# Two heads of transposed probabilities in one DMA transpose, in a decoder layer on one core

## The chip, the core and the metric

The kernel runs on one core of a Trainium2 chip. The metric is the device time of one execution, in microseconds (us), on that core. The kernel before takes 2261.62 us in the median of three runs. The engines are called PE (TensorE matmul), PEld (its weight loads), DVE (VectorE), ACT (ScalarE), POOL (GpSimd) and SP (SyncE, which here issues every DMA).

## The reference

One decoder layer, for 32 batches of 256 tokens of width 256: a causal self-attention with 8 query heads of 128 and one shared key and value head (stage a), a cross-attention with 16 heads of 16 (stage b), and a feed-forward part with 8 gated experts of which the 2 best count, and a shared one (stage c).

```python
x = x + _L0_attn_ref(_layernorm(x), Wq, Wk, Wv, Wo)
x = x + _L0_xattn_ref(_layernorm(x), ctx, ctx, fside, fside, mask, fside_SxS, ...)
x = x + _L0_ffn_ref(_layernorm(x), gate_w, lb_bias, w1, w2, cfc, cproj)

# _L0_xattn_ref, for each batch and each of H = 16 heads of D = 16:
scores = jnp.einsum('bhtd,bhsd->bhts', q, k) * scale
scores = scores + attn_mask[None, None, :, :]
scores = jnp.where(pad, -jnp.inf, scores)
scores = scores + spatial_bias + directional_bias
probs = jax.nn.softmax(scores, axis=-1)
out = jnp.einsum('bhts,bhsd->bhtd', probs, v)
```

## The kernel before

The batches go through the three stages in a software pipeline. Each engine has a list in `ORDERS`, written out by hand, of steps `name:argument@lag`; the engine walks through its list once for each iteration, and a step with lag L works on the batch of L iterations ago. So one iteration of each list is one batch's worth of work from stages a, b and c of different batches, and its length sets the time: 32 batches, and six more iterations in which the pipeline fills and empties. Between the engines there are only semaphores.

In the cross-attention a head j of a batch goes this way, with 256 x 256 probabilities:

- PE makes the scores (`b_s`), DVE adds the bias and takes the negative maximum (`b_s`, line 838), ACT takes the exponential into a PSUM bank (`b_s`, lines 656 and 658).
- ACT rounds it to float16, the "hi" part (`b_p_hi`, line 666), and DVE writes the remainder, the "lo" part (`b_p_lo`, line 845), both into slot `j % DEPTH` of `b_p2` (`DEPTH = 4`).
- SP issues a DMA transpose of the slot, 128 partitions x 1024 columns of float16 (256 KB), into slot `head % RING` of `b_pT` (`RING = 4`); the step is `b_pT:j`, the function `b_pT_load`, line 423. Ahead of it SP waits for DVE's remainder and for PE's product of the head four before, which has read that slot.
- PE multiplies the transposed probabilities with the values (`b_pv:j`, line 1115, 12 small matmuls), once the transpose has landed.
- ACT, when it comes to head j + 4, waits for the landing of head j's transpose ahead of `b_p_hi`, for it writes the same slot of `b_p2`.

After `b_pv:15` DVE divides by the sums (`b_n`, line 857), PE projects the output (`b_o`, `b_wo`), and the layer norm of stage c follows, which the expert products (`c_f1`, `c_f2`) wait for. In PE's list `b_pv:14` and `b_pv:15` stand side by side.

SP's list holds, beside the 16 transposes of a batch, its other DMAs: eight loads of bias (512 KB each, `b_load`), the loads of x and of the context, the store of the result (`c_f2:8`), and, at the end of a batch, the store of q (`b_store_q`, line 390) and k (`b_store_k`, line 383) into a scratch in DRAM and 16 loads that stack them again. All run in one queue (q1). `b_pT:15` has lag 5 and stands at the head of the list, behind `b_store_q`; `b_load:7` and the context's load (`b_split_q`) are the last steps of the list, so that they are issued just ahead of it.

Of the kernel before, what the change touches and what calls it, by code (L numbers as in the profile page):

```python
# [31 lines left out]
BH, BD = 16, 16  # L32
# [4 lines left out]
DEPTH = 4  # L37
RING = 4
# [28 lines left out]
def order(text):  # L67
# [6 lines left out]

ORDERS = {name: order(text) for name, text in dict(
    sync="""
        b_store_q:0@4 b_pT:15@5 b_store_k:0@4 b_stack_q:0@4 b_stack_k:0@4 b_pT:0@4 c_f2:8@6 b_pT:1@4 b_load:0@4
        b_mask:0@4 b_load:1@4 b_pT:2@4 a_ln:0@3 b_pT:3@4 b_load:2@4 b_pT:4@4 b_pT:5@4 b_pT:6@4 b_load:3@4
        b_pT:7@4 b_pT:8@4 b_pT:9@4 b_load:4@4 b_load:5@4 b_pT:10@4 b_pT:11@4 b_load:6@4 a_T:0@2 w_load:4@2
        w_load:5@2 w_load:6@2 w_load:7@2 w_load:8@2 w_load:9@2 w_load:10@2 w_load:11@2 w_load:12@2 w_load:13@2  # L80
        w_load:14@2 w_load:15@2 w_load:16@2 w_load:17@2 w_load:18@2 w_load:19@2 b_pT:12@4 b_pT:13@4 b_pT:14@4
        b_load:7@4 b_split_q:0@3""",
    gpsimd="""
        c_f1:1@6 c_lo:1@6 b_res:0@5 c_f1:2@6 c_lo:2@6 b_comb:6@5 c_f1:3@6 b_comb:7@5 c_lo:3@6 c_f1:4@6
        b_comb:8@5 b_comb:9@5 c_lo:4@6 c_f1:5@6 b_comb:10@5 b_comb:11@5 c_lo:5@6 b_comb:12@5 a_ln:0@3
# [51 lines left out]
def build(nc, x_d, ctx_d, bias_d, mask_d, pad_d, wpair_d, cst_d, bq_d, bk_d, bv_d, bo_d, lb_d, stk_d, out_d):  # L137
    with ExitStack() as ctx:
        def sb(name, shape, dt=F32):
            return ctx.enter_context(nc.sbuf_tensor(name, shape, dt))  # L140
# [4 lines left out]
        def sem(name):  # L145
            return ctx.enter_context(nc.semaphore(name))
# [12 lines left out]
        b_mask = sb("b_mask", [P, CT * T])  # L159
# [58 lines left out]
        b_p2 = sb("b_probs_hi_lo", [P, DEPTH, CT, 2, T], F16)  # L218
        b_pT = sb("b_probsT_hi_lo", [P, RING, CT, 2, CT, P], F16)
# [62 lines left out]
        b_s_ps, b_t_ok, b_e_ok = sem("b_scores_in_psum"), sem("b_neg_scores_ready"), sem("b_exp_ready")  # L282
        b_i_ok = sem("b_inv_ready")
        b_ph_ok, b_p_ok = sem("b_probs_hi_ready"), sem("b_probs_hi_lo_ready")
        b_pT_ok = [sem(f"b_probsT_loaded{n}") for n in range(RING)]
        b_pv_ps, b_of_ok, b_oT_ps = sem("b_pv_in_psum"), sem("b_out_ready"), sem("b_oT_in_psum")
        b_oh_ok, b_o_ok = sem("b_oT_hi_ready"), sem("b_oT_ready")
        b_res_ok, b_wo_ps, x2_ok = sem("x1_bo_ready"), sem("b_wo_in_psum"), sem("x2_ready")
# [36 lines left out]
        def _(sp):  # L325
# [92 lines left out]
            def b_pT_load(b, j):  # L418

                head = b * BH + j  # L420
                sp.wait_ge(b_p_ok, head + 1)
                sp.wait_ge(b_pv_ps, max(head + 1 - RING, 0))
                sp.dma_start_transpose(b_pT[:, head % RING, :, :, :, :].rearrange("p c r s t -> p (c r s) t"),
                                       b_p2[:, j % DEPTH, :, :, :].rearrange("p c r t -> p (c r t)")).then_inc(
                                           b_pT_ok[head % RING], 16)

            def b_mask_row(b, _):

# [4 lines left out]
            def c_f2(b, e):  # L433
                if e == NX - 1:
# [3 lines left out]
            iterations(sp, "sync", dict(w_load=w_load, a_ln=a_ln, a_T=a_T, b_load=b_load, b_split_q=b_split_q,  # L438
                                b_mask=b_mask_row, c_f2=c_f2, b_store_k=b_store_k, b_store_q=b_store_q,
                                b_stack_k=b_stack_k, b_stack_q=b_stack_q, b_pT=b_pT_load))  # L440
            sp.wait_ge(s_out, 16 * BATCHES)

# [109 lines left out]
        def _(act):  # L552
# [16 lines left out]
            def ln_xn(st, x):  # L569
                def step(b, _):  # L570
                    L = ln[st]
                    act.wait_ge(s_nmr[st], after(b, 1, 1))
                    act.wait_ge(s_lnT[st], after(b, 1, 0))
                    for c in range(CT):
                        act.activation(L["xn"][:, c, :], x[:, c, :], ACT.Identity, bias=L["nmr"][:, c:c + 1],
                                       scale=L["rstd"][:, c:c + 1]).then_inc(s_xn[st], 1)
                return step

            def ln_hi(st, free_sem, per_batch):
                def step(b, _):  # L580
                    L = ln[st]
                    act.wait_ge(s_lnT[st], after(b, 1, 1))
                    act.wait_ge(free_sem, after(b, per_batch, 0))
                    act.activation(L["hi"][:, :, :], ln_bank[st][:, :].rearrange("p (k t) -> p k t", k=CD),
                                   ACT.Copy).then_inc(s_xh[st], 1)
                return step
# [74 lines left out]
            def b_p_hi(b, j):  # L661
                act.wait_ge(b_e_ok, after(b, BH, j + 1))
                free = b * BH + j - DEPTH
                if free >= 0:
                    act.wait_ge(b_pT_ok[free % RING], 16 * (free // RING + 1))
                act.activation(b_p2[:, j % DEPTH, :, 0, :], ps_bp[:, :].rearrange("p (c t) -> p c t", c=CT),  # L666
                               ACT.Copy).then_inc(b_ph_ok, 1)

# [17 lines left out]
            def c_sq(b, e):  # L686
# [5 lines left out]
                                           a_T=ln_hi("a", a_q_ps, 4), b_T=ln_hi("b", b_q_ps, 1), c_T=ln_hi("c", c_f1_ps, NX),  # L692
                                 a_ln=ln_xn("a", x_ln), b_ln=ln_xn("b", x1), c_ln=ln_xn("c", x2),
                                 a_kv=a_kv, a_q=a_q_hi, a_s=a_s, a_n=a_n, a_pt=a_pt, a_pv=a_pv, b_kv=b_kv, b_q=b_q,
                                 b_v=b_v_hi, b_s=b_s, b_p=b_p_hi, b_o=b_o_hi, c_gate=c_gate, c_f1=c_f1, c_sq=c_sq))


# [265 lines left out]
        def _(pe):  # L963
# [140 lines left out]

            def b_pv(b, j):
                u = (b * BH + j) % RING
                pe.wait_ge(b_pT_ok[u], 16 * ((b * BH + j) // RING + 1))
                if j == 0:
                    pe.wait_ge(x2_ok, after(b, 1, 0))
                    pe.wait_ge(b_vl_ok, after(b, 1, 1))  # L1110
                for c in range(CT):
                    at = c * D + j * BD
                    for s in range(CT):
                        for n, (part, v) in enumerate([(0, b_vh), (0, b_vl), (1, b_vh)]):
                            last = pe.matmul(ps_bm[:, at:at + BD], b_pT[:, u, c, part, s, :],  # L1115
                                             v[:, s, j * BD:(j + 1) * BD], start=(s == 0 and n == 0),
                                             stop=(s == CT - 1 and n == 2))
                last.then_inc(b_pv_ps, 1)
# [37 lines left out]
            def c_f2(b, e):  # L1156
# [6 lines left out]
                for c in range(CT):  # L1163
# [78 lines left out]
```

## Time and profile before

| what | value |
|---|---|
| time, median of 3 runs | 2261.62 us (2259.73 to 2263.55) |
| the profiled execution | 2262.71 us, of which its span is 2260.9 us |
| PE, PEld busy | 92%, 80% |
| ACT, DVE, POOL busy | 90%, 82%, 79% |
| DMA queue q1, share of 16 engines | 72.4% |
| mean granted TensorE clock | 0.980 |

A share is an average over the whole span. PE is busy nine tenths of it, and in a trace of matmuls that overlap this does not mean that it works at its peak. What ends the small waits between its work has to be read from the views that list waits, and from the order of time within one batch.

### The profile page before, as it was taken

How to read it: one execution, taken by the hardware profiler on the slowest of the kernel's cores; microseconds unless marked ns; L12 is line 12 of the kernel's file. 1: busy time of each engine (PE TensorE's matmuls, PEld its weight loads, DVE VectorE, ACT ScalarE, POOL GpSimd, SP SyncE). 2: the span in 40 equal slices, each digit the busy share in tenths (PEclk: the TensorE clock that was granted, in tenths of full speed). 3: DMA queues.
4: the chain of work that ended last, by engine and by line, in shares of the span. 5: the costliest groups of instructions: out<-in, count | busy, mean ns of one | idle time of the engine just before them, and what ended most of it. 6: DMA issues, size and time to landing. Idle time of an engine off the chain costs nothing.

```text
span 2260.9 us, 73067 instructions
## 1 busy us (share of the span) xinstructions
PE 2077.8 (92%) x24128; PEld 1806.0 (80%) x24128; DVE 1860.7 (82%) x6768; ACT 2024.0 (90%) x5937; POOL 1780.8 (79%) x1899
## 2 busy tenths in 40 slices
PE   4679999999999999999999999999999999999877
PEld 2568888888888888888888888888888888888755
DVE  4578888888888888888888888888888888888763
ACT  5689999999999999999999999999999999999862
POOL 2358888888888887888888888888888888777863
PEclk9789999999999999999999999999999999999987
DMA  4388778778877779767776887677788777789860
GB/s 142 114 191 175 159 156 172 162 170 188 172 157 154 175 157 175 183 162 169 163 173 156 182 185 164 165 169 169 161 176 187 159 168 165 169 152 183 172 129 15
DMA packets 711784, 367.16 MB, mean 162 GB/s; under 512 B 561392, under 2 KB 659952, under 8 KB 711408
## 3 DMA queue, kind: packets, MB, share of 16 engines
q1 hardware_dynamic: 711408, 362.50, 72.4%
q8 instruction: 193, 3.16, 0.6%
q14 instruction: 183, 1.50, 0.2%
HBM read 202.98 MB, written 25.17 MB: 101 GB/s over the span
## 4 chain that ended last, share of the span: by engine, by line
PE 61%; issue 11%; POOL 10%; ACT 8%; DMA 5%; DVE 5%; SPq 1%; ACTq 0%; DVEq 0%; POOLq 0%
PE ps_c_hidden L978 15%; PE ps_a_misc L978 14%; PE ps_c_out L978 14%; PE ps_b_misc L1115 5%; DMA b_probsT_hi_lo<-b_probs_hi_lo 5%; PE ps_b_scores L1101 3%; POOL bias L522 3%; PE ps_a_misc L1057 3%; ACT c_relu L684 2%; PE ps_a_scores L1038 2%; ACT ps_b_probs L658 2%; POOL ctxT_hi L488 2%; ACT a_qT_hi L603 1%; POOL a_qT_lo L480 1%; POOL ctxT_lo L491 1%
## 5 line engine op out<-in xcount | busy, mean ns | idle before, releaser
L522 POOL TENSOR_TENSOR bias<-bias,b_mask 128x512 f32<-128x512 f32 x512 | 645.0, 1274 | 6.2 <-DMA bias<-in_bias 5.8
L838 DVE CUSTOM_DVE_ANT_0 b_neg_scores<-ps_b_scores,bias 128x256 f32<-128x256 f32 x1024 | 391.2, 419 | 68.3 <-POOL bias L522 34.2
L845 DVE TENSOR_TENSOR b_probs_hi_lo<-ps_b_probs,b_probs_hi_lo 128x512 f16<-128x512 f32 x512 | 351.7, 687 | 107.3 <-ACT b_probs_hi_lo L666 104.9
L543 POOL TENSOR_TENSOR c_hidden_lo<-c_hidden,c_hidden_hi 128x512 f16<-128x512 f32 x288 | 335.1, 1163 | 48.4 <-issue 32.8
L978 PE MATMUL ps_c_hidden<-c_xT_hi,w_hi 128*128 128x256 f16 x1152 | 317.2, 275 | 19.9 <-ACT c_relu L684 19.9
L536 POOL TENSOR_TENSOR c_hidden<-c_relu 128x512 f32<-128x512 f32 x288 | 299.7, 1041 | 32.4 <-ACT c_relu L684 13.1
L978 PE MATMUL ps_c_out<-w_hi,c_hidden_hi 128*128 128x256 f16 x1152 | 315.6, 274 | 9.9 <-DVE acc L949 9.9
L978 PE MATMUL ps_c_hidden<-c_xT_hi,w_lo 128*128 128x256 f16 x1152 | 316.8, 275 | 0.0
L978 PE MATMUL ps_c_hidden<-c_xT_lo,w_hi 128*128 128x256 f16 x1152 | 316.7, 275 | 0.0
L978 PE MATMUL ps_c_out<-w_hi,c_hidden_lo 128*128 128x256 f16 x1152 | 315.9, 274 | 0.0
L978 PE MATMUL ps_c_out<-w_lo,c_hidden_hi 128*128 128x256 f16 x1152 | 315.8, 274 | 0.0
L666 ACT ACTIVATE b_probs_hi_lo<-ps_b_probs 128x512 f16<-128x512 f32 x512 | 303.3, 592 | 9.3
L656 ACT ACTIVATE ps_b_probs<-b_neg_scores,b_neg_max 128x256 f32<-128x256 f32 x512 | 245.5, 480 | 55.2 <-DVE b_probs_hi_lo L845 51.1
L658 ACT ACTIVATE ps_b_probs<-b_neg_scores,b_neg_max 128x256 f32<-128x256 f32 x512 | 240.0, 469 | 0.0
L480 POOL TENSOR_TENSOR a_qT_lo<-a_qT,a_qT_hi 128x512 f16<-128x512 f32 x128 | 148.5, 1160 | 115.2 <-ACT a_qT_hi L603 111.8
L949 DVE SCALAR_TENSOR_TENSOR acc<-ps_c_out,g_weights,acc 128x256 f32<-128x256 f32 x512 | 220.7, 472 | 21.6 <-PE ps_c_out L978 21.6
L1115 PE MATMUL ps_b_misc<-b_v_hi,b_probsT_hi_lo 128*128 128x16 f16 x4096 | 218.0, 170 | 21.1 <-DMA b_probsT_hi_lo<-b_probs_hi_lo 21.0
L1115 PEld LDWEIGHTS ps_b_misc<-b_v_hi,b_probsT_hi_lo 128*128 128x128 f16 x4096 | 203.4, 96 | 26.9 <-DMA b_probsT_hi_lo<-b_probs_hi_lo 22.7
L1115 PE MATMUL ps_b_misc<-b_v_lo,b_probsT_hi_lo 128*128 128x16 f16 x2048 | 194.7, 169 | 0.0
L689 ACT ACTIVATE c_hidden_hi<-c_relu 128x512 f16<-128x512 f32 x288 | 180.9, 628 | 6.9 <-PE ps_c_out L978 6.8
L684 ACT ACTIVATE c_relu<-ps_c_hidden 128x512 f32<-128x512 f32 x288 | 170.7, 593 | 14.5 <-PE ps_c_hidden L978 14.5
L978 PE MATMUL ps_a_misc<-a_xT_hi,w_hi 128*128 128x256 f16 x576 | 159.5, 277 | 11.4 <-DVE a_v_lo L752 6.1
(194 smaller groups left out, 7491.0 us busy)
## 6 DMA issues: line engine op xcount, KB each, us to landing
bias<-in_bias SPq DMA_DIRECT2D x256, 512.0 KB, 4.2
q_stack<-qk_scratch SPq DMA_DIRECT2D x256, 64.0 KB, 2.5
x_ln<-in_x SPq DMA_DIRECT2D x32, 256.0 KB, 4.4
ctxT<-in_ctx SPq DMA_DIRECT2D x32, 256.0 KB, 4.4
x<-in_x SPq DMA_DIRECT2D x32, 256.0 KB, 5.5
qk_scratch<-b_qT_hi_lo SPq DMA_DIRECT2D x32, 256.0 KB, 4.5
qk_scratch<-b_kT_hi_lo SPq DMA_DIRECT2D x32, 256.0 KB, 3.7
k_stack_even<-qk_scratch SPq DMA_DIRECT2D x128, 64.0 KB, 2.5
```

The lines of the kernel that those rows point to most:

```text
L522: gp.tensor_tensor(part, part, b_mask[:, :], ALU.add).then_inc(b_c_ok, 1)
L536: gp.tensor_tensor(c_h[:, :], c_r[:, e % 2, :], c_r[:, e % 2, :], ALU.mult).then_inc(c_sq_ok, 1)
L543: gp.tensor_tensor(c_hl[:, u, :], c_h[:, :], c_hh[:, u, :], ALU.subtract).then_inc(c_h_ok, 1)
L656: act.activation(ps_bp[:, 0:T], b_t[:, u, 0, :], ACT.Exp, bias=b_mx[:, u, 0:1], scale=-1.0, accum_out=b_sum[:, 0, j:j + 1])
L658: act.activation(ps_bp[:, T:2 * T], b_t[:, u, 1, :], ACT.Exp, bias=b_mx[:, u, 1:2], scale=-1.0, accum_out=b_sum[:, 1, j:j + 1]).then_inc(b ...
L666: act.activation(b_p2[:, j % DEPTH, :, 0, :], ps_bp[:, :].rearrange("p (c t) -> p c t", c=CT), ACT.Copy).then_inc(b_ph_ok, 1)
L684: act.activation(c_r[:, e % 2, :], ps_c1[:, :], ACT.Relu, scale=R_UP / W_UP).then_inc(c_r_ok, 1)
L838: last = dve.tensor_tensor_reduce(out=b_t[:, u, c, :], in0=ps_bs[:, c * T:(c + 1) * T], in1=bias[:, slot, at:at + T], scale=-2.0, scalar=3 ...
L845: dve.tensor_tensor(b_p2[:, j % DEPTH, :, 1, :], ps_bp[:, :].rearrange("p (c t) -> p c t", c=CT), b_p2[:, j % DEPTH, :, 0, :], ALU.subtrac ...
L949: last = dve.scalar_tensor_tensor(out=acc[:, c, :], in0=ps_c2[:, c * D:(c + 1) * D], scalar=g_we[:, c, e - 1:e], in1=acc[:, c, :], op0=ALU ...
L978: last = pe.matmul(out, stat(s, k), mov(m, k), start=(k == 0 and n == 0), stop=(k == chunks - 1 and n == len(parts) - 1))
L1115: last = pe.matmul(ps_bm[:, at:at + BD], b_pT[:, u, c, part, s, :], v[:, s, j * BD:(j + 1) * BD], start=(s == 0 and n == 0), stop=(s == CT ...
```

## The change

Two neighbouring heads, 2m and 2m + 1, go in one DMA transpose of 128 partitions x 2048 columns. SP's list keeps the odd steps `b_pT:1` to `b_pT:15` where they stood and drops the even ones. The semaphore `b_pT_ok` is one for a pair of slots, two in all in place of four. `b_pv` of either head of a pair, and `b_p_hi` of the heads four later, wait for the pair.

```diff
     sync="""
-        b_store_q:0@4 b_pT:15@5 b_store_k:0@4 b_stack_q:0@4 b_stack_k:0@4 b_pT:0@4 c_f2:8@6 b_pT:1@4 b_load:0@4
...
-        w_load:14@2 w_load:15@2 w_load:16@2 w_load:17@2 w_load:18@2 w_load:19@2 b_pT:12@4 b_pT:13@4 b_pT:14@4
-        b_load:7@4 b_split_q:0@3""",
+        b_store_q:0@4 b_pT:15@5 b_store_k:0@4 b_stack_q:0@4 b_stack_k:0@4 c_f2:8@6 b_pT:1@4 b_load:0@4
...
+        w_load:17@2 w_load:18@2 w_load:19@2 b_pT:13@4 b_load:7@4 b_split_q:0@3""",
...
-        b_pT_ok = [sem(f"b_probsT_loaded{n}") for n in range(RING)]
+        b_pT_ok = [sem(f"b_probsT_loaded{n}") for n in range(RING // 2)]
...
                 head = b * BH + j
+                pair = head // 2 % (RING // 2)
                 sp.wait_ge(b_p_ok, head + 1)
                 sp.wait_ge(b_pv_ps, max(head + 1 - RING, 0))
-                sp.dma_start_transpose(b_pT[:, head % RING, :, :, :, :].rearrange("p c r s t -> p (c r s) t"),
-                                       b_p2[:, j % DEPTH, :, :, :].rearrange("p c r t -> p (c r t)")).then_inc(
-                                           b_pT_ok[head % RING], 16)
+                sp.dma_start_transpose(b_pT[:, 2 * pair:2 * pair + 2, :, :, :, :].rearrange("p u c r s t -> p (u c r s) t"),
+                                       b_p2[:, j % DEPTH - 1:j % DEPTH + 1, :, :, :].rearrange("p u c r t -> p (u c r t)")).then_inc(
+                                           b_pT_ok[pair], 16)
...
-                    act.wait_ge(b_pT_ok[free % RING], 16 * (free // RING + 1))
+                    act.wait_ge(b_pT_ok[free // 2 % (RING // 2)], 16 * (free // RING + 1))
...
-                pe.wait_ge(b_pT_ok[u], 16 * ((b * BH + j) // RING + 1))
+                pe.wait_ge(b_pT_ok[u // 2], 16 * ((b * BH + j) // RING + 1))
```

SP at the end of a batch, before: the three transposes in one row are those of heads 12, 13 and 14, the single one is that of head 15, and between them stand the last load of bias, the load of the context and the store of q.

```order
L361 DMA x_ln<-in_x 128x512 [waits a_xT_in_psum]
L423 DMA_TRANSPOSE b_probsT_hi_lo<-b_probs_hi_lo 128x8x128 [waits b_pv_in_psum,b_probs_hi_lo_ready] x3
L370 DMA bias<-in_bias 128x1024 [waits b_neg_scores_ready]
L376 DMA ctxT<-in_ctx 128x512 [waits ctx_lo_ready]
L390 DMA qk_scratch<-b_qT_hi_lo 128x4x256 [waits b_q_lo,b_q_stack_loaded]
L423 DMA_TRANSPOSE b_probsT_hi_lo<-b_probs_hi_lo 128x8x128 [waits b_pv_in_psum,b_probs_hi_lo_ready]
L383 DMA qk_scratch<-b_kT_hi_lo 128x4x256 [waits b_k_lo,b_k_stack_loaded]
```

The same place in the changed kernel:

```order
L360 DMA x_ln<-in_x 128x512 [waits a_xT_in_psum]
L423 DMA_TRANSPOSE b_probsT_hi_lo<-b_probs_hi_lo 128x16x128 [waits b_pv_in_psum,b_probs_hi_lo_ready]
L369 DMA bias<-in_bias 128x1024 [waits b_neg_scores_ready]
L375 DMA ctxT<-in_ctx 128x512 [waits ctx_lo_ready]
L389 DMA qk_scratch<-b_qT_hi_lo 128x4x256 [waits b_q_lo,b_q_stack_loaded]
L423 DMA_TRANSPOSE b_probsT_hi_lo<-b_probs_hi_lo 128x16x128 [waits b_pv_in_psum,b_probs_hi_lo_ready]
L382 DMA qk_scratch<-b_kT_hi_lo 128x4x256 [waits b_k_lo,b_k_stack_loaded]
```

Head 14 has moved from ahead of the bias, context and q transfers to behind them, and the load of bias no longer stands behind a transpose that waits for head 14's remainder.

ACT in the middle of a batch, before; `b_probsT_loaded` is the semaphore of the slot's transpose, and the rows left out are other stages' steps:

```order
L666 ACTIVATE b_probs_hi_lo<-ps_b_probs 128x2x256 [waits b_probsT_loaded0,b_exp_ready]
...
L666 ACTIVATE b_probs_hi_lo<-ps_b_probs 128x2x256 [waits b_probsT_loaded1,b_exp_ready]
...
L666 ACTIVATE b_probs_hi_lo<-ps_b_probs 128x2x256 [waits b_probsT_loaded2,b_exp_ready]
L684 ACTIVATE c_relu<-ps_c_hidden 128x512 [waits c_hidden_hi_ready,c_square_ready,c_hidden_in_psum]
...
L666 ACTIVATE b_probs_hi_lo<-ps_b_probs 128x2x256 [waits b_probsT_loaded3,b_exp_ready]
```

The same rows in the changed kernel:

```order
L666 ACTIVATE b_probs_hi_lo<-ps_b_probs 128x2x256 [waits b_probsT_loaded0,b_exp_ready]
...
L666 ACTIVATE b_probs_hi_lo<-ps_b_probs 128x2x256 [waits b_probsT_loaded0,b_exp_ready]
...
L666 ACTIVATE b_probs_hi_lo<-ps_b_probs 128x2x256 [waits b_probsT_loaded1,b_exp_ready]
L684 ACTIVATE c_relu<-ps_c_hidden 128x512 [waits c_hidden_hi_ready,c_square_ready,c_hidden_in_psum]
...
L666 ACTIVATE b_probs_hi_lo<-ps_b_probs 128x2x256 [waits b_probsT_loaded1,b_exp_ready]
```

No step of ACT has moved; the first head of a pair now waits for a transpose that starts with the second head's remainder, one head later than before.

## Rows read from the trace of the kernel before

**Rows 1.** The page: the chain that ended last, by engine, shares of the span.

```profile
PE 61%; issue 11%; POOL 10%; ACT 8%; DMA 5%; DVE 5%; SPq 1%; ACTq 0%; DVEq 0%; POOLq 0%
```

**Rows 2.** Waits of the whole span: total us, times, longest us.

```profile
PE ps_b_misc L1115 <- DMA b_probsT_hi_lo<-b_probs_hi_lo: 21.0, 18, 2.1
```

**Rows 3.** DVE's line 851, once per batch, in batches 7, 8, 19, 20: ns, then start.

```profile
L851 DVE RECIPROCAL b_inv<-b_sum x1: 349/349/349, 615.7 to 615.7; 128x32 f32<-128x32 f32 x1
L851 DVE RECIPROCAL b_inv<-b_sum x1: 346/346/346, 683.3 to 683.3; 128x32 f32<-128x32 f32 x1
L851 DVE RECIPROCAL b_inv<-b_sum x1: 350/350/350, 1412.4 to 1412.4; 128x32 f32<-128x32 f32 x1
L851 DVE RECIPROCAL b_inv<-b_sum x1: 348/348/348, 1478.0 to 1478.0; 128x32 f32<-128x32 f32 x1
```

**Rows 4.** Timeline of PE, first matmul of `b_pv:15` of batch 7; in brackets, idle time ahead.

```profile
624.48 0.18 PE L1115 MATMUL ps_b_misc<-b_v_hi,b_probsT_hi_lo 128*128 128x16 f16 x1 [1.91 <-DMA b_probsT_hi_lo<-b_probs_hi_lo]
```

**Rows 5.** Timeline of SP, end of batch 16: transposes of heads 13, 14, 15 and between.

```profile
1210.67 1.24 SPq L423 DMA_TRANSPOSE b_probsT_hi_lo<-b_probs_hi_lo  x1
...
1213.39 1.78 SPq L423 DMA_TRANSPOSE b_probsT_hi_lo<-b_probs_hi_lo  x1
1215.22 0.57 SPq L370 DMA_DIRECT2D bias<-in_bias  x1
1215.85 0.42 SPq L376 DMA_DIRECT2D ctxT<-in_ctx  x1
1216.40 0.38 SPq L390 DMA_DIRECT2D qk_scratch<-b_qT_hi_lo  x1
1216.88 1.50 SPq L423 DMA_TRANSPOSE b_probsT_hi_lo<-b_probs_hi_lo  x1
```

**Rows 6.** Timeline of PE, batch 16: first matmuls of `b_pv:14` and of `b_pv:15`.

```profile
1221.72 0.17 PE L1115 MATMUL ps_b_misc<-b_v_hi,b_probsT_hi_lo 128*128 128x16 f16 x1
...
1222.34 0.18 PE L1115 MATMUL ps_b_misc<-b_v_hi,b_probsT_hi_lo 128*128 128x16 f16 x1 [0.17 <-DMA b_probsT_hi_lo<-b_probs_hi_lo]
```

**Rows 7.** All transposes: ns min/median/max of the issue; us from issue to landing.

```profile
L423 SPq DMA_TRANSPOSE b_probsT_hi_lo<-b_probs_hi_lo x512: 1231/1252/3742, 111.4 to 2204.7; - x171
...
DMA to landing us min/median/max: 3.0/3.5/7.9
```

**Rows 8.** Landing of head 15's transpose alone, in batch 19, then in batch 7.

```profile
DMA to landing us min/median/max: 4.8/4.8/4.8
DMA to landing us min/median/max: 7.4/7.4/7.4
```

**Rows 9.** DMA issues: KB each, median us from issue to landing.

```profile
bias<-in_bias SPq DMA_DIRECT2D x256, 512.0 KB, 4.2
...
x_ln<-in_x SPq DMA_DIRECT2D x32, 256.0 KB, 4.4
...
qk_scratch<-b_qT_hi_lo SPq DMA_DIRECT2D x32, 256.0 KB, 4.5
qk_scratch<-b_kT_hi_lo SPq DMA_DIRECT2D x32, 256.0 KB, 3.7
```

**Rows 10.** Timelines of DVE and POOL, batch 16: head 15's scores and remainder; q's remainder.

```profile
1212.24 0.42 DVE L838 CUSTOM_DVE_ANT_0 b_neg_scores<-ps_b_scores,bias 128x256 f32<-128x256 f32 x1
1215.54 0.68 DVE L845 TENSOR_TENSOR b_probs_hi_lo<-ps_b_probs,b_probs_hi_lo 128x512 f16<-128x512 f32 x1
1214.94 1.16 POOL L505 TENSOR_TENSOR b_qT_hi_lo<-b_qT,b_qT_hi_lo 128x512 f16<-128x512 f32 x1 [1.44 <-issue]
```

**Rows 11.** Timelines, batch 16: SP's transpose of head 7, ACT's head 10.

```profile
1194.32 1.38 SPq L423 DMA_TRANSPOSE b_probsT_hi_lo<-b_probs_hi_lo  x1
...
1199.19 0.60 ACT L666 ACTIVATE b_probs_hi_lo<-ps_b_probs 128x512 f16<-128x512 f32 x1
```

**Rows 12.** Timelines, batch 16: SP's transpose of head 11, PE's first matmul of head 10.

```profile
1205.96 1.23 SPq L423 DMA_TRANSPOSE b_probsT_hi_lo<-b_probs_hi_lo  x1
...
1211.25 0.17 PE L1115 MATMUL ps_b_misc<-b_v_hi,b_probsT_hi_lo 128*128 128x16 f16 x1
```

More of the change, by code:

```diff
@@ L76 @@
     sync="""
-        b_store_q:0@4 b_pT:15@5 b_store_k:0@4 b_stack_q:0@4 b_stack_k:0@4 b_pT:0@4 c_f2:8@6 b_pT:1@4 b_load:0@4
-        b_mask:0@4 b_load:1@4 b_pT:2@4 a_ln:0@3 b_pT:3@4 b_load:2@4 b_pT:4@4 b_pT:5@4 b_pT:6@4 b_load:3@4
-        b_pT:7@4 b_pT:8@4 b_pT:9@4 b_load:4@4 b_load:5@4 b_pT:10@4 b_pT:11@4 b_load:6@4 a_T:0@2 w_load:4@2
-        w_load:5@2 w_load:6@2 w_load:7@2 w_load:8@2 w_load:9@2 w_load:10@2 w_load:11@2 w_load:12@2 w_load:13@2
-        w_load:14@2 w_load:15@2 w_load:16@2 w_load:17@2 w_load:18@2 w_load:19@2 b_pT:12@4 b_pT:13@4 b_pT:14@4
-        b_load:7@4 b_split_q:0@3""",
+        b_store_q:0@4 b_pT:15@5 b_store_k:0@4 b_stack_q:0@4 b_stack_k:0@4 c_f2:8@6 b_pT:1@4 b_load:0@4
+        b_mask:0@4 b_load:1@4 a_ln:0@3 b_pT:3@4 b_load:2@4 b_pT:5@4 b_load:3@4 b_pT:7@4 b_pT:9@4 b_load:4@4
+        b_load:5@4 b_pT:11@4 b_load:6@4 a_T:0@2 w_load:4@2 w_load:5@2 w_load:6@2 w_load:7@2 w_load:8@2
+        w_load:9@2 w_load:10@2 w_load:11@2 w_load:12@2 w_load:13@2 w_load:14@2 w_load:15@2 w_load:16@2
+        w_load:17@2 w_load:18@2 w_load:19@2 b_pT:13@4 b_load:7@4 b_split_q:0@3""",
     gpsimd="""
```

## The prediction

> **What bounds the kernel now.** I read the chain that ended last first, because five engines between 79% and 92% busy do not say which of them waits for what. It is PE for 61% of the span, and DMA for 5% [rows 1]; the reader is to see there that a transfer stands on the path at all, 5% of 2260.9 us being 113 us, or 3.5 us in each of 32 batches. The view of waits then says which: PE's product of probabilities and values waits for the DMA transpose 18 times, 21.0 us in all, 2.1 us at most [rows 2]. Eighteen times in 32 batches is about once in every second batch, so I looked for one head of the 16 at which it happens, and it is head 15.
>
> Whether such a wait costs time is read from the length of a batch. In batch 19 no such wait stands, and DVE's line 851 comes again after 1478.0 - 1412.4 = 65.6 us; in batch 7 PE waits 1.91 us ahead of `b_pv:15`, and the next line 851 comes after 683.3 - 615.7 = 67.6 us [rows 3, 4]. The batch is longer by 2.0 us, all of the wait. It is paid in full: DVE's division, the output projection and stage c's layer norm follow head 15's product.
>
> Why head 15: SP issues its transpose at 1216.88, right behind the load of bias (512 KB), the load of the context and the store of q, three transfers within 1.7 us [rows 5]. PE starts `b_pv:14` at 1221.72, 4.84 us after that issue. `b_pv:15` starts at 1222.34 after 0.17 us of waiting; it could have started at 1222.17, 5.29 us after the issue, 0.45 us behind `b_pv:14` [rows 6]. A transpose lands after 3.0 us at best and 3.5 us in the median [rows 7]; head 15's took 4.8 us in batch 19, which is in time, and 7.4 us in batch 7, which is not [rows 8].
>
> **The change part by part.** *A longer transfer.* The issue of 8 blocks of 128 columns takes 1.23 to 1.25 us where nothing holds it up [rows 7]. No row shows 16 blocks. The nearest row for an upper bound is that issue: if blocks are made one after the other, a pair's last block leaves, and lands, 1.24 us later. The nearest for the lower bound are plain loads, where 512 KB land after 4.2 us and 256 KB after 4.4 [rows 9]: twice the bytes, no time. An issue of plain transfers takes 0.38 to 0.57 us whatever their size [rows 5], so a transpose's 1.24 us cannot be a fixed cost of issuing alone. I take 1.24 us and keep 0 for the range.
>
> *A weighing.* The Trainium skill ("DMA: Bandwidth & Descriptors", section "Anatomy of one DMA", fitted there on GpSimd's path) gives one transfer a fixed 2.0 us and its bytes over 436 GB/s, and its section "Rules for kernel authors" says to join small transfers. By that the second 256 KB would add an estimated 0.6 us in place of 1.24, and the sum below would be +4.5 us in place of +21.6. The trace's 3.0 us for the shortest transpose is above the 2.6 us that the formula gives for 256 KB.
>
> *Less traffic just ahead.* Head 14's transpose, which now leaves from 1213.39 to 1215.17, goes; the load of bias and the context's load, which stand behind it, need only the scores of head 15, done at 1212.66, and a free queue [rows 5, 10]. The pair 12, 13 is issued when head 13's is now, at 1210.67, and holds the queue for 2.5 us by the price above, to 1213.15. So both loads leave about 2.0 us earlier than at 1215.22 and 1215.85. The store of q does not: POOL's remainder of q ends at 1216.10 [rows 10], 0.3 us ahead of the store's issue. It then has almost no traffic in front. What that is worth shows in two stores of the same size: q's lands after 4.5 us, k's, behind a gap, after 3.7 [rows 9]. So 0.8 us. Bounds: nothing, and 1.45 us, the amount by which the slower 4.5 us exceeds the shortest transpose of 3.0 us.
>
> *Head 14 waits for head 15.* This is the edit's price on the path. Now `b_pv:14` is done before `b_pv:15` may start; after it, both wait for one landing and run one behind the other, so that `b_pv:15` starts 0.45 us after the landing [rows 6]. The pair's issue cannot move forward, for head 15's remainder ends at 1216.22 [rows 10], behind which only the store of q stands.
>
> *The sum at this place.* In the 18 batches that wait [rows 2]: 0.45 + 1.24 - 0.8 = 0.89 us more, 16.0 us in all. In the other 14: a landing of 4.8 us [rows 8] becomes 5.24 us, 0.40 us over the 4.84 us at which PE wants `b_pv:14`, 5.6 us in all. Together +21.6 us.
>
> *The other pairs,* with 1.24 us on top of their odd head's landing. ACT's head 10 writes the slot of head 6, whose pair is issued with head 7's transpose at 1194.32 and lands, by the median 3.5 us, at 1199.06; ACT starts at 1199.19 [rows 7, 11]. It is covered by 0.13 us, thin cover; without it, each us that the landing is late stops ACT, and PE's expert products want its rectified values next. PE's head 10 is wanted at 1211.25, and its pair, issued with head 11's at 1205.96, lands at 1210.70 [rows 7, 12]; the cover is 0.55 us. Landings scatter (3.0 to 7.9 us), so these two lose a little: an estimate of 0.1 us a batch, 3 us in all. The same issue order frees SP at the end of batches such as 16, where head 15's transpose left 0.66 us after the remainder it needs (1216.88 - 1216.22), of which 0.3 us is the store of q that the queue held up; at 0.3 us in a third of the batches that is 3 us back. I set these two against each other. SP's other issues keep their order, and a queue that now waits in fewer places costs nothing that a row shows.
>
> Against the profiled execution, 2262.71 us, of which 2260.9 is the span, the sum is 2284.3 us; that execution stands 1.1 us over the median of the three runs, so the forecast is 2283 us.
>
> **The rivals.** *Faster: the queue clears.* If the pair lands no later than one head does today (0 for the longer transfer) and the loads' head start is worth 0.8 us, each waiting batch wins 0.8 - 0.45 = 0.35 us, 6 us in all; with 1.45 us it wins 1.0 us, 18 us, of the 21.0 us that there are. Between them, 2250 us. It decides at a landing 4.84 us after the issue: if most pairs are there by then, PE waits at neither head. For it: the plain loads in rows 9. Against: the issue time in rows 7.
>
> *The same:* a longer transfer at about 0.5 us, between the bounds. Each waiting batch then costs 0.45 + 0.5 - 0.8 = 0.15 us, 2.7 us in all, and the others 4.8 - 0.3 = 4.5 us, in time: 2264 us. The formula cited above would give nearly this.
>
> *Much slower: no relief.* If head 15's landing is late for something other than the loads in front, it stays, and all of 0.45 + 1.24 = 1.69 us comes on top in 18 batches (30 us), and 4.8 + 1.24 - 4.84 = 1.2 us in 14 (17 us): 2309 us. For it: 4.8 us in one batch and 7.4 us in another behind the same three transfers [rows 8], which a queue of fixed length does not explain. With ACT's head 10 late by 0.5 us in every batch it would be 16 us more.
>
> **How the numbers follow.** Forecast, slower by about 1%: 0.45; much slower: 0.17; the same: 0.18; faster: 0.20. A change of 0.2%, 4.5 us, is about what a measurement of this kernel can tell from none. So faster 0.20, same 0.18, slower 0.62. The range runs from the middle of the faster case, 2250 us, to the much slower case and a little of ACT's share, 2315 us; the likeliest case alone spans 2270 to 2298 us, a transfer price of 0.9 to 1.5 us.
>
> **What would show it.** Right: an issue of about 2.5 us for 16 blocks; PE's waits for the transpose rise from 21 us to about 43, in most batches, now ahead of `b_pv:14`; the store of q lands after about 3.7 us; batches of 65.6 us become rare. Wrong: an issue well under 2 us, or pairs of heads 14 and 15 that land within 4.8 us. New waits of ACT's line 666 for the transpose would mean that the slots of `b_p2`, not PE's last heads, set the price.

## The result and the profile after

The changed kernel takes 2309.97 us (2304.36 to 2311.97, 4 runs), the kernel before, run beside it, 2261.77 us: a ratio of 1.0209, 95% interval 1.019 to 1.0229. It is slower by 48 us, where 21 had been forecast. The profiled execution took 2309.93 us with a span of 2308.1.

The page of the changed kernel, chain that ended last, by engine:

```profile
PE 41%; DMA 15%; issue 13%; POOL 12%; ACT 11%; DVE 7%; SPq 1%; DVEq 0%; ACTq 0%; POOLq 0%
```

DMA stood at 5% [rows 1] and now holds 15% of the path. The waits of the changed kernel (us in all, times, longest) say whose:

```profile
PE ps_b_misc L1115 <- DMA b_probsT_hi_lo<-b_probs_hi_lo: 47.6, 40, 3.7
DVE b_out L857 <- PE ps_b_misc L1115: 43.7, 31, 3.8
ACT b_probs_hi_lo L666 <- DMA b_probsT_hi_lo<-b_probs_hi_lo: 14.4, 16, 1.6
```

PE waits 47.6 us for the transposes in place of 21.0 [rows 2], and ACT has a wait that it did not have at all, for the slots of `b_p2`. (DVE's 43.7 us, 23.9 before, are ahead of its division, line 857, which waits for the last product: in the main the same waits, seen one step on.) PE's and ACT's together are 62.0 us against 21.0, a rise of 41 us; the span rose by 47.2. Sorted by head, from the idle time ahead of each head's first matmul in PE's timeline: before, 19.2 us ahead of head 15 and 1.8 ahead of head 12; now 35.3 ahead of head 14, 5.9 ahead of head 10, 5.0 ahead of head 12, 1.4 ahead of head 2. ACT's 14.4 us stand ahead of head 10 (12.1), 6 and 14.

All pairs of the changed kernel: ns min/median/max of the issue, then us from issue to landing.

```profile
L423 SPq DMA_TRANSPOSE b_probsT_hi_lo<-b_probs_hi_lo x256: 1317/2670/5212, 113.8 to 2252.0; - x128
...
DMA to landing us min/median/max: 4.2/4.9/8.4
```

The shortest landing rose from 3.0 to 4.2 us [rows 7], by 1.2 us, near the 1.24 of the forecast. The shortest issue barely rose, from 1231 to 1317 ns, but the median is 2670 ns, more than two single issues of 1252. Summed over the trace, the transposes' issues take 678 us in place of 743: half as many issues in nine tenths of the time. What had been two issues, apart from each other, now stands in one piece where only the second had stood.

The end of batch 12 of the changed kernel, timeline of SP from pair 12, 13 to pair 14, 15, and below it PE's first matmul of `b_pv:14`:

```profile
965.91 3.20 SPq L423 DMA_TRANSPOSE b_probsT_hi_lo<-b_probs_hi_lo  x1
969.16 0.58 SPq L369 DMA_DIRECT2D bias<-in_bias  x1
969.78 0.43 SPq L375 DMA_DIRECT2D ctxT<-in_ctx  x1
971.25 0.38 SPq L389 DMA_DIRECT2D qk_scratch<-b_qT_hi_lo  x1
971.73 4.49 SPq L423 DMA_TRANSPOSE b_probsT_hi_lo<-b_probs_hi_lo  x1
...
977.89 0.18 PE L1115 MATMUL ps_b_misc<-b_v_hi,b_probsT_hi_lo 128*128 128x16 f16 x1 [0.97 <-DMA b_probsT_hi_lo<-b_probs_hi_lo]
```

In this batch the load of bias leaves 2.57 us ahead of the last transpose. Over batches 1 to 30 the median is 3.0 us, in the kernel before 2.0: 1.0 us earlier, not the 2.0 of the forecast, in the main because the issue of pair 12, 13 takes 3.3 us in the median (3.20 here) and not 2.5. PE takes up `b_pv:14` 6.16 us after the issue, with a wait of 0.97 us ahead of it; in batch 16 of before it started after 4.84 us without one [rows 6].

One long wait, batch 22 of the changed kernel: PE's first matmul of `b_pv:14` in the timeline, and DVE's line 851 ahead of it and in the next batch, by its line.

```profile
1647.71 0.19 PE L1115 MATMUL ps_b_misc<-b_v_hi,b_probsT_hi_lo 128*128 128x16 f16 x1 [3.50 <-DMA b_probsT_hi_lo<-b_probs_hi_lo]
```

```profile
L851 DVE RECIPROCAL b_inv<-b_sum x1: 349/349/349, 1637.5 to 1637.5; 128x32 f32<-128x32 f32 x1
L851 DVE RECIPROCAL b_inv<-b_sum x1: 345/345/345, 1709.6 to 1709.6; 128x32 f32<-128x32 f32 x1
```

Line 851 of the next batch starts at 1709.6, 72.1 us later: 6.5 us over the 65.6 of a batch without a wait [rows 3], for a wait of 3.5. A single long wait can cost more than itself, and here the granted clock of TensorE accounts for the rest. The same batch in four stretches, PE alone (start and end, us, PE's busy time and instructions, granted clock as a share of 2.4 GHz, DMA share, GB/s): up to the wait, the wait, behind it, the rest.

```profile
1637.50:1644.21 6.71, 6.71 (x84) 1.00 1.15 249
1644.21:1647.71 3.50, 0.01 (x2) 0.87 0.80 203
1647.71:1653.62 5.91, 5.91 (x52) 0.50 0.50 137
1653.62:1709.60 55.98, 53.90 (x624) 1.00 0.64 146
```

The clock falls to its lower level, 1.2 GHz, while PE waits, and stays there for 5.91 us after the wait. If PE's work takes twice as long there, that is an estimated 3.0 us on top of the 3.5, which together are the 6.5. The same view from 200 to 2100 us, that is, without the pipeline's filling and emptying, before and after the change:

```profile
200.00:2100.00 1900.00, 1822.29 (x21599) 1.00 0.77 168
200.00:2100.00 1900.00, 1799.23 (x21162) 0.99 0.74 165
```

In that stretch the kernel before has no time at 1.2 GHz at all. The changed kernel has five falls, 24 us together, each one in or within 2 us behind a wait of 1.6 to 3.5 us for the last pair: an estimate of up to 12 us lost, beside the waits themselves.

DMA issues of the changed kernel (KB each, median us to landing), those of [rows 9]:

```profile
bias<-in_bias SPq DMA_DIRECT2D x256, 512.0 KB, 4.4
...
x_ln<-in_x SPq DMA_DIRECT2D x32, 256.0 KB, 4.7
...
qk_scratch<-b_qT_hi_lo SPq DMA_DIRECT2D x32, 256.0 KB, 3.6
qk_scratch<-b_kT_hi_lo SPq DMA_DIRECT2D x32, 256.0 KB, 3.4
```

The store of q lands after 3.6 us in place of 4.5, as forecast from k's 3.7: the traffic ahead of it did thin out.

### The profile page after: what moved, and what is told of

Read it like the earlier page. It is cut to its first block, busy times and chain, and to the rows that moved or that the text cites. A ratio compares the mean times of both kernels' runs of the same rounds, so it can differ in the third digit from the quotient of the medians.

```text
span 2308.1 us, 72555 instructions
## 1 busy us (share of the span) xinstructions
PE 2094.8 (91%) x24128; PEld 1807.4 (78%) x24128; DVE 1862.1 (81%) x6768; ACT 2025.2 (88%) x5937; POOL 1780.6 (77%) x1899
## 4 chain that ended last, share of the span: by engine, by line
PE 41%; DMA 15%; issue 13%; POOL 12%; ACT 11%; DVE 7%; SPq 1%; DVEq 0%; ACTq 0%; POOLq 0%
DMA b_probsT_hi_lo<-b_probs_hi_lo 14%; PE ps_c_hidden L978 10%; PE ps_c_out L978 9%; PE ps_a_misc L978 8%; POOL bias L522 4%; PE ps_b_misc L1115 4%; PE ps_b_scores L1101 2%; ACT c_relu L684 2%; PE ps_a_misc L1057 2%; ACT ps_b_probs L658 2%; ACT ps_b_probs L656 2%; DVE b_neg_scores L838 2%; ACT a_qT_hi L603 1%; POOL b_qT_hi_lo L505 1%; POOL ctxT_hi L488 1%
## 5 line engine op out<-in xcount | busy, mean ns | idle before, releaser
L536 POOL TENSOR_TENSOR c_hidden<-c_relu 128x512 f32<-128x512 f32 x288 | 299.7, 1041 | 31.5 <-ACT c_relu L684 12.1
L666 ACT ACTIVATE b_probs_hi_lo<-ps_b_probs 128x512 f16<-128x512 f32 x512 | 303.2, 592 | 23.6 <-DMA b_probsT_hi_lo<-b_probs_hi_lo 14.4
L1115 PE MATMUL ps_b_misc<-b_v_hi,b_probsT_hi_lo 128*128 128x16 f16 x4096 | 216.2, 170 | 48.0 <-DMA b_probsT_hi_lo<-b_probs_hi_lo 47.6
```

The costliest lines, as they stand in the source:

```text
L536: gp.tensor_tensor(c_h[:, :], c_r[:, e % 2, :], c_r[:, e % 2, :], ALU.mult).then_inc(c_sq_ok, 1)
```

## The experiments

In these kernels a list `SPLIT` names the pairs (0 for heads 0 and 1, to 7 for heads 14 and 15) whose two heads are moved singly again, each in its old place of SP's list and on a semaphore of its own; `landed(head)` gives the semaphore and count that a head's readers wait for. Every time is a median beside runs of the kernel before on the same chip, 2261 to 2263 us.

**First question: which pair costs.** Theory A put the loss at the last pair, as the forecast did; rival B at the seven others.

*Heads 14 and 15 single again, the others joined.*

```diff
+SPLIT = [7]
...
-        w_load:17@2 w_load:18@2 w_load:19@2 b_pT:13@4 b_load:7@4 b_split_q:0@3""",
+        w_load:17@2 w_load:18@2 w_load:19@2 b_pT:13@4 b_pT:14@4 b_load:7@4 b_split_q:0@3""",
...
+                if j // 2 in SPLIT:
+                    sp.dma_start_transpose(b_pT[:, head % RING, :, :, :, :].rearrange("p c r s t -> p (c r s) t"),
+                                           b_p2[:, j % B_DEPTH, :, :, :].rearrange("p c r t -> p (c r t)")).then_inc(
+                                               landed(head)[0], 16)
+                    return
```

> Heads 14 and 15 go in two transposes again, head 14 ahead of the last load of bias as in the kernel before; the other seven pairs stay joined. Theory A (the loss of 48 us sits at the last pair, where head 14 has been put behind three other transfers and its product behind one landing): about 29 us come back, 2275 to 2285 us, and PE's waits for the transpose fall from 47.6 to 25 to 32 us. Rival B (a joined transfer costs about the same wherever it stands, through ACT's slots and PE's other heads): no more than an eighth to a quarter comes back, 2298 us or over.

Measured: 2297.02 us, ratio 1.0139 (1.0118 to 1.016). PE waits 38.4 us, of them 26.1 at head 15; ACT 14.6. Most of the loss is still there; the time is 12 us above theory A's range and 1 us below rival B's.

*Only heads 14 and 15 joined.*

```diff
+SPLIT = [0, 1, 2, 3, 4, 5, 6]
```

> The other way round: only heads 14 and 15 are joined, the other 14 heads go singly in the places that they have in the kernel before. Theory A: nearly all of its share, 2285 to 2297 us, with PE waiting for head 14 in most batches. Rival B: 2262 to 2272 us.

Measured: 2270.86 us, ratio 1.0036 (1.0017 to 1.0055); PE waits 24.0 us, ACT none. The last pair alone costs about 8 us, and PE's wait at head 14 is 22.8 us, only 3.6 more than head 15's before. Theory A falls: the other seven cost 34 us by the run above. The two together are 42 of the 48 us; the rest comes only when all pairs are joined.

*Two single transposes, one behind the other, at each odd head's place.* This keeps the place and the bytes of the joined transfer, but the first head's landing is told on its own.

```diff
+                    for n in (j - 1, j):
+                        sp.dma_start_transpose(b_pT[:, (b * BH + n) % RING, :, :, :, :].rearrange("p c r s t -> p (c r s) t"),
...
```

> At the place of every joined transpose, and after the same waits, two single ones are issued one behind the other, each with its own semaphore; so both heads still wait for the second, and the same bytes go at the same time, but the first head's landing is told on its own. Theory A, in the form that the place in the queue counts: head 14 is still behind the other transfers; only the 0.45 us of its product and the first halves' later landings come back, 2275 to 2292 us. Rival C (the one landing for two heads is the whole cost, the place nothing): 2262 to 2270 us.

Measured: 2290.34 us, ratio 1.0112 (1.0093 to 1.0132); PE waits 33.9 us (head 14 19.7, head 15 10.1), ACT 2.1. Rival C falls: with the one landing for two heads taken away, 27 of the 48 us stay. This run leaves two things as they were in the changed kernel, the even head's transpose held back to the odd head's place and the two transfers in one row, and does not tell one from the other. ACT's wait at head 10 goes from 12.1 to 0.6 us, PE's from 5.9 to none: these were waits of an even head for the joint landing.

*Pairs 3 and 7 split (heads 6, 7, 14 and 15).*

```diff
+SPLIT = [3, 7]
```

> As e1_last_split, and the pair of heads 6 and 7 is split too, so that ACT's head 10 waits for head 6 alone, which is issued one load earlier. Theory A with ACT's 14.4 us of waits for the transpose as a cost in full: 8 to 14 us under e1_last_split. If ACT has slack there: within 4 us of e1_last_split.

Measured: 2289.84 us (2277.98 to 2297.56), ratio 1.0101 (1.0067 to 1.0135). In the profiled run, one of the long ones (2297.18), ACT's wait at head 10 is gone, and PE's at head 15 is 31.6 us. Against the first run ACT waits 10.5 us less and PE 5.6 us more, so that in this run half of what pair 3 gave back was lost again. By the medians 7 us are won against the first run, a little under the 8 to 14 of the theory, where the runs lie 20 us apart.

**Second question: why head 15 waits more when heads 10 to 13 are joined.** In the first run above head 15's own transpose was single again, yet its wait was 26.1 us in place of 19.2.

*Pairs 6 and 7 split: heads 12 to 15 single as before the change.*

```diff
+SPLIT = [6, 7]
```

> The transposes of heads 12 to 15 are single again, those of heads 0 to 11 are joined as in the changed kernel. Theory, each joined pair costs where its own slack is short: the end of the batch is then as before (the loads of bias and context leave about 2 us ahead of head 15's issue, PE's waits at heads 12 and 15 about 21 us), and what is left is PE's head 10 and head 2 (some 7 us of waits) and ACT's head 10 (12 us), so PE waits about 28 us, ACT about 12 us, and the time is 2275 to 2285 us. Rival, any joined transfer holds up the one queue and with it all that follows, head 15 too: PE's waits stay at 35 us or more and the time at 2290 us or more.

Measured: 2297.41 us, ratio 1.0153 (1.0113 to 1.0194); PE waits 39.0 us, head 15 32.0 of it; ACT 11.9. The rival holds: a joined pair costs far behind itself.

*Only heads 0 to 5, 8 and 9 joined.*

```diff
+SPLIT = [3, 5, 6, 7]
```

> Only heads 0 to 5, 8 and 9 are joined (four pairs); 6, 7 and 10 to 15 are single as before the change. ACT's slot for head 10 and PE's heads 10, 12, 14 and 15 then hang on single transposes. Theory, a joined pair costs only where its slack is short: PE waits 21 to 24 us, ACT none, and the time is 2260 to 2268 us, level with the kernel before. Rival, any joined transfer costs through the shared queue: about 5 us for each pair, so 2275 to 2285 us.

Measured: 2264.89 us, ratio 1.0034 (1.0011 to 1.0056); PE waits 17.9 us, ACT 2.4. Within the theory's range, though the interval says a loss of 0.1 to 0.6%. So it is not any pair; pairs 3 and 5 make the difference.

*Only heads 10 and 11 joined.*

```diff
+SPLIT = [0, 1, 2, 3, 4, 6, 7]
...
-        b_pT:7@4 b_pT:8@4 b_pT:9@4 b_load:4@4 b_load:5@4 b_pT:10@4 b_pT:11@4 b_load:6@4 a_T:0@2 w_load:4@2
+        b_pT:7@4 b_pT:8@4 b_pT:9@4 b_load:4@4 b_load:5@4 b_pT:11@4 b_load:6@4 a_T:0@2 w_load:4@2
```

(The lines taken away and added are of the kernel before.)

> Only heads 10 and 11 are joined; the fourteen others are single, in the order of the kernel before. Theory, the queue on SP has no slack between head 11 and head 15: the pair's issue takes 0.7 us more than head 11's, all that follows on SP moves back, and head 15's wait grows from 19 us to about 30 although nothing of head 15 changed; with 5 us of PE's waits at head 10 that is 2272 to 2280 us. Rival, a pair costs only at its own heads: 5 us at head 10, head 15 as before, 2262 to 2268 us.

Measured: 2291.76 us, ratio 1.0123 (1.0101 to 1.0145): one joined pair of eight costs 28 us, more than the theory's 11 to 19 (30 us by the medians). Head 15's wait is 32.1 us, head 10's 5.0, ACT has none. The timeline of SP in batch 18 of this kernel (start, us of the issue), from the pair to head 15:

```profile
1346.26 2.03 SPq L442 DMA_TRANSPOSE b_probsT_hi_lo<-b_probs_hi_lo  x1
1348.33 0.91 SPq L383 DMA_DIRECT2D bias<-in_bias  x1
1349.29 0.44 SPq L374 DMA_DIRECT2D x_ln<-in_x  x1
1349.83 1.24 SPq L438 DMA_TRANSPOSE b_probsT_hi_lo<-b_probs_hi_lo  x1
1351.17 2.57 SPq L438 DMA_TRANSPOSE b_probsT_hi_lo<-b_probs_hi_lo  x1
1353.83 2.19 SPq L438 DMA_TRANSPOSE b_probsT_hi_lo<-b_probs_hi_lo  x1
1356.07 0.57 SPq L383 DMA_DIRECT2D bias<-in_bias  x1
1356.69 0.51 SPq L389 DMA_DIRECT2D ctxT<-in_ctx  x1
1357.34 0.38 SPq L403 DMA_DIRECT2D qk_scratch<-b_qT_hi_lo  x1
1357.82 1.48 SPq L438 DMA_TRANSPOSE b_probsT_hi_lo<-b_probs_hi_lo  x1
```

The same stretch of the kernel before, the same batch, from head 11 to head 15:

```profile
1337.48 1.23 SPq L423 DMA_TRANSPOSE b_probsT_hi_lo<-b_probs_hi_lo  x1
1338.77 0.57 SPq L370 DMA_DIRECT2D bias<-in_bias  x1
1339.39 0.43 SPq L361 DMA_DIRECT2D x_ln<-in_x  x1
1340.40 1.25 SPq L423 DMA_TRANSPOSE b_probsT_hi_lo<-b_probs_hi_lo  x1
1342.19 2.00 SPq L423 DMA_TRANSPOSE b_probsT_hi_lo<-b_probs_hi_lo  x1
1344.91 1.23 SPq L423 DMA_TRANSPOSE b_probsT_hi_lo<-b_probs_hi_lo  x1
1346.19 0.57 SPq L370 DMA_DIRECT2D bias<-in_bias  x1
1346.81 0.62 SPq L376 DMA_DIRECT2D ctxT<-in_ctx  x1
1347.72 0.38 SPq L390 DMA_DIRECT2D qk_scratch<-b_qT_hi_lo  x1
1348.20 1.80 SPq L423 DMA_TRANSPOSE b_probsT_hi_lo<-b_probs_hi_lo  x1
```

Count from the first row of each. The pair's issue is 0.80 us longer, the load of bias behind it 0.34; layer norm's x leaves 1.12 us later, and behind it the issues of heads 13 and 14 take 2.57 and 2.19 us in place of 2.00 and 1.23. SP has no idle time left here: from 1349.83 to 1356.07 one issue follows the other, where there were gaps of 0.58, 0.54 and 0.72 us. The two loads end their issue 0.99 us later (10.94 us after the first row in place of 9.95), the store of q leaves 0.84 us later, and so does head 15's transpose, at 11.56 us in place of 10.72. It is the late issue that counts: over batches 1 to 30 head 15's transpose leaves 1.03 us after the remainder that it needs, 0.55 before (means), and then lands after 5.75 us, as before (5.73). The transposes' waits rise by 17 of the 28 us. Of the rest, the clock is a part: between 200 and 2100 us it falls to 1.2 GHz five times, 17 us in all, each time in or within 2 us behind a wait at head 15 of 1.7 us or more, an estimate of up to 8.5 us.

*Only heads 6 and 7 joined.*

```diff
+SPLIT = [0, 1, 2, 4, 5, 6, 7]
```

> Only heads 6 and 7 are joined; the others are single. Theory, what this pair costs is ACT's head 10, which overwrites head 6's slot: ACT waits 10 to 12 us there, PE's waits are those of the kernel before (21 us), and the time is 2270 to 2276 us. Rival, ACT's wait is taken up by the slack behind it: the wait shows, and the time stays at 2259 to 2264 us.

Measured: 2276.24 us, ratio 1.0078 (1.0051 to 1.0106). Waits of this kernel:

```profile
ACT b_probs_hi_lo L685 <- DMA b_probsT_hi_lo<-b_probs_hi_lo: 16.4, 19, 2.0
PE ps_b_misc L1134 <- DMA b_probsT_hi_lo<-b_probs_hi_lo: 14.8, 17, 2.4
```

The theory's mechanism holds against the rival: the slot wait is paid for, all of it at head 10, which overwrites head 6. Its numbers were missed: ACT's wait is 16.4 us for 10 to 12, PE's 14.8 for 21, and the time stands just above its range.

**Third question: is a wait paid one for one, and does the cause lie in the loads ahead of the last transpose.**

*The kernel before, with the loads of bias and context behind head 15's transpose in SP's list.*

```diff
-        b_store_q:0@4 b_pT:15@5 b_store_k:0@4 b_stack_q:0@4 b_stack_k:0@4 b_pT:0@4 c_f2:8@6 b_pT:1@4 b_load:0@4
+        b_store_q:0@4 b_pT:15@5 b_load:7@5 b_split_q:0@4 b_store_k:0@4 b_stack_q:0@4 b_stack_k:0@4 b_pT:0@4 c_f2:8@6 b_pT:1@4 b_load:0@4
...
-        w_load:14@2 w_load:15@2 w_load:16@2 w_load:17@2 w_load:18@2 w_load:19@2 b_pT:12@4 b_pT:13@4 b_pT:14@4
-        b_load:7@4 b_split_q:0@3""",
+        w_load:14@2 w_load:15@2 w_load:16@2 w_load:17@2 w_load:18@2 w_load:19@2 b_pT:12@4 b_pT:13@4 b_pT:14@4""",
```

> The kernel before, with single transposes; in SP's list the loads of bias and context for the next batch stand right behind head 15's transpose instead of ahead of it. Theory, the loads in front make head 15's landing late: its median landing falls from 5.2 us to below 4.5, PE's waits for it from 19 us to below 8, and the time is 2240 to 2252 us. Rival, the late landings have another cause: PE's waits stay at 15 us or more and the time at 2258 to 2264 us. If the loads are now late for the next batch, a new wait for bias or context shows and the time is above 2265 us.

Measured: 2245.23 us, ratio 0.9934 (0.9912 to 0.9957): faster than both kernels, and the theory's number. Its waits for transposes, the end of batch 16 on SP's timeline, and the landing of the transpose seen there:

```profile
PE ps_b_misc L1114 <- DMA b_probsT_hi_lo<-b_probs_hi_lo: 1.2, 1, 1.2
```

```profile
1208.81 0.39 SPq L389 DMA_DIRECT2D qk_scratch<-b_qT_hi_lo  x1
1209.29 1.29 SPq L422 DMA_TRANSPOSE b_probsT_hi_lo<-b_probs_hi_lo  x1
1210.64 0.57 SPq L369 DMA_DIRECT2D bias<-in_bias  x1
1211.26 0.42 SPq L375 DMA_DIRECT2D ctxT<-in_ctx  x1
```

```profile
DMA to landing us min/median/max: 3.3/3.3/3.3
```

With the loads behind it, head 15's transpose lands after 3.3 us, and PE waits for head 15 in no batch; the one wait left stands ahead of head 12. The chain of this kernel has 1% of DMA.

*The same move in the changed kernel.*

> The changed kernel with the same move: the loads of bias and context behind the transpose of heads 14 and 15. Theory, the loads in front make the last landing late: pair 14 and 15 lands after about 4.5 us in place of 6.2, PE's waits at head 14 fall from 35 us to about 10, and the time is 2275 to 2290 us. Rival, the pair's own length and other traffic set it: the waits at head 14 stay at 25 us or more and the time at 2300 to 2312 us.

Measured: 2294.23 us, ratio 1.0145 (1.0116 to 1.0174), 16 us below the changed kernel but over the theory's range: head 14's wait falls from 35.3 to 16.6 us, not to 10, and the other waits stay (12.6 at PE, 15.5 at ACT).

*Heads 0 to 11 joined, 12 to 15 single, loads behind.*

> Heads 0 to 11 joined and 12 to 15 single, as in the run that had 2297 us and 32 us of waits at head 15, now with the loads of bias and context behind head 15's transpose. Theory, waits for transposes are paid one for one: the 32 us go, about 17 us at heads 10, 2 and 12 and in ACT stay, and the time is the 2245 us of the single transposes with the loads behind, plus 17 to 20: 2260 to 2268 us. Rival, the waits are only the place where a busy queue shows, and what goes at head 15 comes back elsewhere: 2275 us or more.

Measured: 2262.55 us, ratio 0.9999 (0.9987 to 1.0011), the theory's time: 35 us less than the same pairs with the loads ahead, of which 32 us stood at head 15. The waits that stay are more than it had, 24 us (PE 9.4, ACT 15.0) for 17, and they cost less than their length: against single transposes with the loads behind, the kernel is 17 us longer by the medians, 12 by the spans.

*Heads 0 to 5, 8 and 9 joined, the rest single, loads behind.*

> Heads 0 to 5, 8 and 9 joined, the rest single, and the loads of bias and context behind head 15's transpose. Theory, these four pairs neither cost nor win, since their issues and landings have slack: 2245 to 2250 us, level with the single transposes with the loads behind (2245), so that the joining itself is worth nothing where it is harmless. Rival, fewer issues free the queue once the end of the batch is relieved: below 2242 us.

Measured: 2253.82 us, ratio 0.9953 (0.9936 to 0.9971): neither. Against single transposes with the loads behind, these four pairs cost 8.6 us by the medians and 4 us by the ratios, whose intervals overlap, so that a cost is likely but not clear of noise here. Fewer issues won nothing in any run.

**The runs together.** The waits of PE and of ACT for transposes, in us, beside the span of the same profiled execution; the last column is 2244.4 us (the span of the table's first kernel without its own 1.2 us of waits) plus the waits.

| kernel | PE | ACT | span | 2244.4 + waits |
|---|---|---|---|---|
| single, loads behind | 1.2 | 0 | 2245.6 | 2245.6 |
| four early pairs, loads behind | 4.5 | 3.4 | 2254.4 | 2252.3 |
| heads 0 to 11 joined, loads behind | 9.4 | 15.0 | 2257.1 | 2268.8 |
| before | 21.0 | 0 | 2260.9 | 2265.4 |
| four early pairs | 17.9 | 2.4 | 2261.3 | 2264.7 |
| only the last pair | 24.0 | 0 | 2268.8 | 2268.4 |
| only heads 6, 7 | 14.8 | 16.4 | 2270.5 | 2275.6 |
| only heads 10, 11 | 38.1 | 0 | 2289.3 | 2282.5 |
| two single issues | 33.9 | 2.1 | 2291.4 | 2280.4 |
| heads 0 to 11 joined | 39.0 | 11.9 | 2293.8 | 2295.3 |
| all joined, loads behind | 29.2 | 15.5 | 2294.2 | 2289.1 |
| pairs 3 and 7 split | 44.0 | 4.1 | 2295.4 | 2292.5 |
| last pair split | 38.4 | 14.6 | 2297.9 | 2297.4 |
| all joined | 47.6 | 14.4 | 2308.1 | 2306.4 |

The sum follows the spans within 12 us over a stretch of 62. In the main, the time of the change is the time that PE and ACT stand before a transpose, and the clock adds to it. In the 14 traces it falls to 1.2 GHz 34 times between 200 and 2100 us. Of these falls 32 come in or within 2.2 us behind a wait of PE of more than 1 us for a transpose, the oftener the longer the wait (4 of 55 waits of 1 to 1.5 us, 12 of 13 of 2.5 us and more).

An estimate of the prices is a fit to the lengths of 378 batches, 27 from each of the 14 traces, with the time lost to the clock taken as half of the time at 1.2 GHz. A batch takes 65.8 us, plus 1.05 times PE's waits for transposes in it, 0.82 times ACT's, and 0.87 times the time lost to the clock; what is left over is 0.3 us (root mean square). So PE's waits are paid one for one and ACT's to four fifths, and the changed kernel's five falls cost some 10 us; a fit without the clock charges PE's waits with 1.44. No run changed the clock by itself, so this is not shown by an experiment. The two largest misses of the sum go the same way: two single issues (11 us more) had 24 us at 1.2 GHz in that stretch, heads 0 to 11 joined with the loads behind (12 us less) none. How much of each miss is the clock stays open.

## Why the prediction fell short

The direction and the kind of cost were right, the size was not: 48 us in place of 21. By its own steps:

- *A longer transfer, 1.24 us.* Right in size: the shortest landing is 4.2 us against 3.0. By the formula of the Trainium skill ("DMA: Bandwidth & Descriptors", "Anatomy of one DMA", fitted on GpSimd's path) it would have been an estimated 0.6 us; the measurement decides, and it is twice that. The reason given for it, that an issue lasts as long as its blocks take, was wrong: 16 blocks can be issued in 1317 ns. So the size came out by luck, as far as is known; what sets it stays open.
- *Less traffic ahead, 0.8 us.* About right in the changed kernel: over batches 1 to 30 the last transpose lands after 5.73 us in the mean before and 6.28 after, 0.55 us more, which is 1.24 less 0.69. The loads' head start was smaller than forecast (1.0 us for 2.0). With only the last pair joined the landing is 5.64 us, no later than before: there the relief was worth all of the longer transfer.
- *Head 14 waits for head 15, 21.6 us at this place.* The place is right, the nearness of the number is luck. PE's waits at the two heads rose from 19.2 to 35.3 us, 16 us. But the last pair by itself, which is what the forecast priced, cost 8 us and 3.6 us of waits; the other 12.5 us of waits here came with the other seven pairs, behind which the last one lands after 6.28 us and not 5.64.
- *The other pairs, 3 us set against 3 us.* This is the step that failed: it gave the seven other pairs nothing, and joined without the last they cost 34 us. At heads 10, 12 and 2 PE waits 12.3 us (1.8 before), at heads 10, 6 and 14 ACT waits 14.4 (none before): 25 us. The covers, 0.13 us at ACT's head 10 and 0.55 us at PE's head 10, were worked out with a median landing, and that was not far off: pair 10, 11 lands after 4.5 us in the median where 4.7 had been assumed. But its landings reach 6.0 us, those of pair 6, 7 6.3 us, and a cover is paid for by the landings beyond it: 13 batches at ACT's head 10, 9 at PE's, spread over 32 batches 0.38 and 0.18 us in place of 0.1 for both. The text had named the price ("16 us more") and the sign to look for (ACT's line 666); it gave them too small a share.
- *"A queue that now waits in fewer places costs nothing."* In the changed kernel SP itself bears this out: from head 11's place to head 15's it issues for 8.0 of 10.7 us in the median (8.3 before), and the last pair leaves 0.47 us after its remainder in the mean (0.55 before), some 2.6 us in all, about the 3 us that the forecast set for it. What it left out is the landing, which the other pairs make longer (above). And it does not hold for pairs ahead of single heads: joining heads 10 and 11 alone cost 28 us, 13 of them in waits at head 15, whose own code had not changed.
- *No term for the clock.* The five falls to 1.2 GHz behind long waits, an estimated 10 us, stand in no step of the forecast.
- *The rival "much slower: no relief"* gave 2309 us, nearly the time measured, but by luck: the relief came, and the time went at the other pairs and into the clock.
- *Two slips in its sums.* A transfer price of 0.9 to 1.5 us gives 2272 to 2292 us by its own terms, not 2270 to 2298, and the bound of 1.45 us is 4.5 - 3.0 = 1.5 by its rows. Neither moves the forecast.

Of the signs named, the waits of about 43 us came as 47.6, ahead of `b_pv:14` as said, and the store of q as said; the issue of 2.5 us came in the median only.

## What to carry to other kernels

A joined transfer starts when its last part is ready and lands later: ask for each of its parts when it was wanted, and set the cover against the longest landings of the trace, not their median. A long wait of PE can cost more than itself: look at the granted clock in and behind it. A queue that is full between two points hands any longer issue on to everything behind it, so a change may be paid at a place that it does not touch. Here what helped was not fewer transfers but the order: two loads wanted only in the next batch, moved behind the transpose that PE was waiting for, took 16 us off the kernel as it was.

## What the runs showed that was not expected

- The shortest issue of a transpose hardly grows with its length (1231 ns for 8 blocks, 1317 for 16), while its shortest landing does (3.0 and 4.2 us). In the median the issue of a pair takes 2.67 us, at most 5.2, and SP issues nothing else meanwhile.
- Two loads of 768 KB in all made a transpose issued right behind them land after 5.4 us in the median of batches 1 to 30; with the same loads right behind it, it landed after 3.4.
- A late last transpose often has a fetch of instructions in its flight. In the kernel before, a packet of the instruction queues fell into 23 of 30 flights, which took 6.0 us in the median; the 7 others took 4.8. A longer flight has more chances to meet one, and no run took the fetches away, so whether they are a cause stays open.
